# Attention and encoder in one kernel: a third exponential buffer, products with v in two halves, normalisation sums on GpSimd

## What is computed

```python
score = einsum('bhsd,bhtd->bhst', qh, kh) / sqrt(8)
attn = softmax(score, axis=-1)
a = einsum('bhst,bhtd->bhsd', attn, vh)      # then [b, 128, 512] reshaped to [b, 512, 128]
x = x + layernorm(a + XN)
```

## Time and profile before

| | us |
|---|---|
| median of three runs | 616.35 |
| the profiled execution | 617.56 |
| its span in the profile | 615.8 |
| TensorE matmul busy | 507.8 (82%) |
| VectorE busy | 525.9 (85%) |
| ScalarE busy | 395.2 (64%) |
| GpSimd busy | 194.5 (32%) |

### The profile page before, as it was taken

How to read it: one execution, slowest core, us unless ns; L and a number is a source line. 1 busy time by engine, 2 the same in 40 slices (tenths; PEclk the granted TensorE clock), 3 DMA queues, 4 the chain that set the end, 5 groups by cost and what they waited for, 6 DMA issues and landing times.

```text
span 615.8 us, 9778 instructions
## 1 busy us (share of the span) xinstructions
PE 507.8 (82%) x3468; PEld 196.9 (32%) x3475; DVE 525.9 (85%) x879; ACT 395.2 (64%) x773; POOL 194.5 (32%) x309
## 2 busy tenths in 40 slices
PE   1866999999999999999999998877578798888500
PEld 1634122222222222222222222256457665433200
DVE  5989799999999999999999994158988669899976
ACT  1753588989898889898888887534446321145252
POOL 7001021259321752045340338149366230000000
PEclk9999599999999999999999999999979799999965
DMA  8944010111220102211121200020000000001012
GB/s 215 304 142 141 17 40 25 36 30 36 70 71 24 41 22 75 56 46 30 33 58 49 60 19 7 6 81 2 2 2 1 1 1 1 1 0 35 2 34 68
DMA packets 31793, 28.94 MB, mean 47 GB/s; under 512 B 6256, under 2 KB 23800, under 8 KB 31744
## 3 DMA queue, kind: packets, MB, share of 16 engines
q1 hardware_dynamic: 29712, 27.33, 15.5%
q10 hardware_dynamic: 2032, 0.98, 0.6%
HBM read 19.23 MB, written 8.65 MB: 45 GB/s over the span
## 4 chain that ended last, share of the span: by engine, by line
PE 45%; DVE 30%; POOL 7%; ACT 6%; issue 4%; DMA 4%; SPq 2%; ACTq 1%; DVEq 0%
PE ps L1490 14%; PE ps L1485 11%; DVE row_max L1677 8%; PE ps L1458 5%; DVE space L925 4%; PE ps L584 2%; DVE space L861 2%; ACT attended L1619 2%; DMA w_in<-in_L_ffn_out_proj_w 1%; ACT space L1603 1%; PE ps L591 1%; DVE st L233 1%; DMA space<-max_turned 1%; ACT space L829 1%; POOL space L401 1%
## 5 line engine op out<-in xcount | busy, mean ns | idle before, releaser
L1677 DVE TENSOR_REDUCE row_max<-ps 128x2 f32<-128x1024 f32 x256 | 299.9, 1219 | 17.1 <-PE ps L1458 14.0
L1603 ACT ACTIVATE space<-ps 128x512 f32<-128x512 f32 x512 | 272.1, 604 | 49.3 <-PE ps L1485 48.8
L1485 PE MATMUL ps<-space 51*128 51x512 bf16 x512 | 158.5, 387 | 6.9 <-ACT space L1603 3.0
L1490 PE MATMUL ps<-space 128*32 128x512 f32 x1024 | 138.0, 611 | 2.9 <-ACT space L1603 0.7
L1458 PE MATMUL ps<-space 48*128 48x512 bf16 x512 | 125.5, 391 | 9.0 <-DVE row_max L1677 7.2
L1485 PEld LDWEIGHTS ps<-space 51*128 51x128 bf16 x512 | 40.8, 94 | 163.8 <-ACT space L1603 143.0
L1333 POOL CAST max_parts<-row_max 128x16 bf16<-128x16 f32 x32 | 6.4, 199 | 231.0 <-DVE row_max L1677 230.9
L584 PE MATMUL ps<-W,space 128*128 128x512 f32 x128 | 65.4, 592 | 0.4
L925 DVE TENSOR_REDUCE space<-ps 128x128 f32<-128x1024 f32 x32 | 38.7, 1220 | 9.7 <-PE ps L584 9.4
L447 POOL TENSOR_TENSOR space<-PC,same_row 128x512 f32<-128x512 f32 x32 | 33.0, 1063 | 35.7 <-DVE PC L875 27.6
L1458 PEld LDWEIGHTS ps<-space 48*128 48x128 bf16 x512 | 26.3, 94 | 49.1 <-DVE row_max L1677 41.0
(11 more groups left out here) (216 smaller groups left out, 624.7 us busy)
## 6 DMA issues: line engine op xcount, KB each, us to landing
space<-q_parts_dram SPq DMA_DIRECT2D x64, 48.0 KB
attended_dram<-attended SPq DMA_DIRECT2D x128, 18.0 KB
X<-in_L_attn_queries SPq DMA_DIRECT2D x8, 256.0 KB, 7.8
space<-in_L_ffn_w SPq DMA_DIRECT2D x2, 1024.0 KB, 6.5
space<-q_parts_dram SPq DMA_DIRECT2D x64, 32.0 KB
space<-attended_dram SPq DMA_DIRECT2D x16, 128.0 KB, 2.5
space<-inverses_dram SPq DMA_DIRECT2D x16, 128.0 KB
out<-space SPq DMA_DIRECT2D x4, 512.0 KB, 3.2
```

The source lines that it names most:

```text
L1485: pe.matmul(ps[:, col_bank(v), :], k_rows[rows_a, kappa // 4 % 2, tc * P:(tc + 1) * P], q_stack[rows_a, kappa % 4, b * S:(b + 1) * S], sta ...
L1490: mm = pe.matmul(ps[32 * m:32 * m + 32, PV, :], v_heads[:, tc, PAIR * (kappa // 4) + m % PAIR, :], probs[:, tc % 2, m, :], start=(tc == 0) ...
L1603: act.activation(probs[:, tc % 2, m, :], ps[:, col_bank(v), :], ACT.Exp, scale=1.0 / math.sqrt(DH)).then_inc(s_pr, 1)
L1677: dve.tensor_reduce(row_max[:, par].rearrange("p (a c) -> p a c", a=PAIR)[:, :, item], ring(n), AX.X, MAX).then_inc(s_free, 1)
```

## The change

`probs` becomes three buffers. TensorE's step moves column item 0 of the next block ahead of the first row products and pairs items 1 and 2; the products with v of a block are done one step later, in two halves of 256 columns (block 0 in one piece of 512), each behind a pair of row matmuls. ScalarE copies bank 7 of slot kappa - 1 after the second exponential of block 1 of slot kappa. Each piece of `first_group` comes one step earlier. SyncE does a slot's own loads first, then the denominators (c = 1), the attended values and the inverses' store (c = 2). For groups 0 and 1 GpSimd sums means and variances itself, by halving additions, in slots c = 5, 6, 8 and 9; group 2 keeps VectorE's bn_stats (at c = 5, and within `first_group_copies`).

```diff
-        probs = view(space4, 0, [2, QB, S])
+        probs = [view(space4, 0, [QB, S]), view(space4, QB * S, [QB, S]), view(space8, 0, [QB, S])]
...
+        def pool_add_up(pool, ch, src, scratch, total):
+            n = D // 2
+            ch.done(pool.tensor_tensor(scratch[:, :, 0:n], src[:, :, 0:n], src[:, :, n:2 * n], ADD))
+            ch.wait()
+            while n > 2:
+                n //= 2
+                ch.done(pool.tensor_tensor(scratch[:, :, 0:n], scratch[:, :, 0:n], scratch[:, :, n:2 * n], ADD))
+                ch.wait()
+            ch.done(pool.tensor_tensor(total.rearrange("p (b o) -> p b o", o=1), scratch[:, :, 0:1],
+                                       scratch[:, :, 1:2], ADD))
+            ch.wait()
+        def pool_centre(pool, ch, src, dst, scratch):
+            mean = smallp[:, 0, :]
+            pool_add_up(pool, ch, src, scratch, mean)
+            ch.done(pool.tensor_scalar(mean, mean, 1.0 / D, None, MUL))
+            ch.wait()
+            ch.done(pool.tensor_tensor(dst, src, over_f(mean), SUB))
+            ch.wait()
+            ch.done(pool.tensor_tensor(scratch, dst, dst, MUL))
+            ch.wait()
+        def pool_scale(pool, ch, dst, scratch):
+            var, inv = smallp[:, 2, :], smallp[:, 3, :]
+            pool_add_up(pool, ch, scratch, scratch, var)
+            ch.done(pool.tensor_scalar(var, var, 1.0 / D, EPS, MUL, ADD))
+            ch.wait()
+            ch.done(pool.tensor_tensor(inv, var, neg_half[:], ALU.pow))
+            ch.wait()
+            return pool.tensor_tensor(dst, dst, over_f(inv), MUL)
...
+        def pool_group(pool, ch, g, c):
+            scratch = XN[:, g]
+            if c == 4:
+                pool_divide(pool, ch, g)
+            if g < G - 2:
+                if c == 5:
+                    pool.wait_ge(s_r1, g + 1)
+                    pool_centre(pool, ch, A[:, g], A[:, g], scratch)
+                if c == 6:
+                    ch.done(pool_scale(pool, ch, A[:, g], scratch))
+                    ch.wait()
...
+            else:
+                if c == 6:
+                    pool.wait_ge(s_st, 1)
+                    ch.done(pool_norm(pool, ch, A[:, g], A[:, g]))
+                    ch.wait()
+                    pool_residual(pool, ch, g)
+                if c == 7:
+                    pool.wait_ge(s_st, 2)
+                    pool_norm(pool, ch, X[:, g], A[:, g]).then_inc(s_n2, 1)
+                    pool_out_bias(pool, g)
...
-            first_group(pe, 7)
...
+            def load_denominators(g):
 
                 for par in range(2):
                     sp.wait_ge(s_ast[par], 64 * 4 * (g + 1))
+                for h in range(NH // G):
+                    den = a_dram[:, g * (NH // G) + h:g * (NH // G) + h + 1, DH:DH + 1, :]
+                    sp.dma_start(den_sb[32 * h:32 * h + 32], den.rearrange("b h o (j f) -> (h o j) b f", f=D)).then_inc(s_dl, 16)
+            def load_attended(g):
...
+                if kappa + 1 < NQ:
+                    sp.wait_ge(s_pr, turn_item(kappa + 1) + 1)
+                    load_shift(kappa + 1)
                 if kappa:
                     sp.wait_ge(s_pve, kappa)
                     store_attended(kappa - 1)
 
-                if kappa + 1 < NQ:
-                    sp.wait_ge(s_pr, turn_item(kappa + 1) + 1)
-                    load_shift(kappa + 1)
             for kappa in range(NQ):
                 g, c = kappa // 8, kappa % 8
+                slot(kappa)
                 if c == 1 and g:
+                    load_denominators(g - 1)
+                if c == 2 and g:
                     load_attended(g - 1)
-                if c == 2 and g:
                     store_inverses(g - 1)
                 if c == 3 and g:
                     load_inverses(g - 1)
-                slot(kappa)
                 if 2 <= kappa < 2 + QB:
                     load_c(kappa - 2)
             sp.wait_ge(s_pve, NQ)
             store_attended(NQ - 1)
+            load_denominators(G - 1)
...
+                if g >= 2:
+                    pool_group(pool, ch, g - 2, c + 8)
                 if g:
-                    if c == 3:
-                        pool_divide(pool, ch, g - 1)
-                    if c == 5:
-                        pool_residual(pool, ch, g - 1)
-                    if c == 7:
-                        pool_input(pool, ch, g - 1)
+                    pool_group(pool, ch, g - 1, c)
...
-            def multiply_v(kappa, tc):
+            def multiply_v(n, half):
+                kappa, tc = n // TC, n % TC
+                if half == 0:
+                    if tc == 0 and kappa:
+                        pe.wait_ge(s_pve, kappa)
+                    pe.wait_ge(s_pr, column_item(kappa, tc, QB - 1) + 1)
+                if tc == 0 and half == 1:
+                    return
+                cols = slice(0, S) if tc == 0 else slice(half * S // 2, (half + 1) * S // 2)
                 for m in range(QB):
-                    mm = pe.matmul(ps[32 * m:32 * m + 32, PV, :], v_heads[:, tc, PAIR * (kappa // 4) + m % PAIR, :],
-                                   probs[:, tc % 2, m, :], start=(tc == 0), stop=(tc == TC - 1))
-                if tc == TC - 1:
+                    mm = pe.matmul(ps[32 * m:32 * m + 32, PV, cols], v_heads[:, tc, PAIR * (kappa // 4) + m % PAIR, :],
+                                   probs[n % 3][:, m, cols], start=(tc == 0), stop=(tc == TC - 1 and half == 1))
+                if tc == TC - 1 and half == 1:
                     mm.then_inc(s_pv, 1)
 
             pe.wait_ge(s_kl[0], 32)
 
             def step(kappa, tc):
 
-                piece = TC * (kappa - (NQ - 2)) + tc - 1
-                if piece >= 0:
-                    first_group(pe, piece)
-                n = 8 * (kappa + 2) + 2 * tc
+                n, row = TC * kappa + tc, 8 * (kappa + 2) + 2 * tc
                 ahead, following = kappa + 2 < NQ, kappa + 1 < NQ
                 score_columns(kappa, tc, 3)
                 if tc == 1 and following:
                     turn_max(kappa + 1)
+                score_columns(kappa, tc + 1, 0)
                 if ahead:
                     if tc == 0:
                         pe.wait_ge(s_ql[(kappa + 2) % 4], 96 * ((kappa + 2) // 4 + 1))
                         if (kappa + 2) % 4 == 0:
                             i = (kappa + 2) // 4
                             pe.wait_ge(s_kl[i % 2], 32 * (i // 2 + 1))
-                    score_rows(n, kappa + 2, 2 * tc)
-                score_columns(kappa, tc + 1, 0)
+                    score_rows(row, kappa + 2, 2 * tc)
+                    if n:
+                        multiply_v(n - 1, 0)
+                else:
+                    first_group(pe, TC * (kappa - (NQ - 2)) + tc)
                 score_columns(kappa, tc + 1, 1)
+                score_columns(kappa, tc + 1, 2)
                 if ahead:
-                    score_rows(n + 1, kappa + 2, 2 * tc + 1)
-                score_columns(kappa, tc + 1, 2)
-                if tc == 0 and kappa:
-                    pe.wait_ge(s_pve, kappa)
-                pe.wait_ge(s_pr, column_item(kappa, tc, QB - 1) + 1)
-                multiply_v(kappa, tc)
+                    score_rows(row + 1, kappa + 2, 2 * tc + 1)
+                else:
+                    multiply_v(n - 1, 0)
+                if n:
+                    multiply_v(n - 1, 1)
 
             for kappa in range(NQ):
                 for tc in range(TC):
                     step(kappa, tc)
+            for half in range(2):
+                multiply_v(TC * NQ - 1, half)
             back_end_pe(pe)
 
         @block.scalar
                 src = ps[0:PARTS * QB * TC, col_bank(v), 0:P // 2].bitcast(BF16)
                 act.copy(max_turned[:, kappa % 2, :], src).then_inc(s_pr, 1)
 
-            def exps(kappa, tc):
-                for m in range(QB):
+            def exps(kappa, tc, which=range(QB)):
+                for m in which:
                     v = column_item(kappa, tc, m)
                     act.wait_ge(s_sc, v + 1)
-                    act.activation(probs[:, tc % 2, m, :], ps[:, col_bank(v), :], ACT.Exp,
+                    act.activation(probs[(TC * kappa + tc) % 3][:, m, :], ps[:, col_bank(v), :], ACT.Exp,
                                    scale=1.0 / math.sqrt(DH)).then_inc(s_pr, 1)
 
-            copy_turned(0)
-            exps(0, 0)
-            for kappa in range(NQ):
-                for tc in range(1, TC):
-                    exps(kappa, tc)
-                    if tc == 1 and kappa + 1 < NQ:
-                        copy_turned(kappa + 1)
-                if kappa + 1 < NQ:
-                    exps(kappa + 1, 0)
+            def copy_attended(kappa):
                 act.wait_ge(s_pv, kappa + 1)
                 if kappa >= 2:
                     act.wait_ge(s_ast[kappa % 2], 64 * (kappa // 2))
                 act.copy(attended[:, kappa % 2, :], ps[:, PV, :]).then_inc(s_pve, 1)
+            copy_turned(0)
+            for kappa in range(NQ):
```

(65 more changed lines are left out.)

## The result

The changed kernel takes 628.52 us in the median of four runs (625.19 to 630.14), the kernel before 616.57 (616.21 to 618.8): ratio 1.0163, 95% interval 1.0132 to 1.0195. Timed again in three rounds on another occasion it is 629.84 against 617.59, ratio 1.0185 (1.0128 to 1.0243). The sign was forecast, the size was not: +12 us against +4.6, and the time lies outside the stated range of 603 to 627 us.

A forecast was written before the change was run, and what follows sets the result against it. The order of work, not an engine's busy time, was taken as the bound; slots +10.4, start -1.2, last two slots -5.2 and encoder +0.6 gave +4.6 us, so 621.0 us, range 603 to 627.

The forecast's parts named there:

- The slot: Attention slots: each takes 10.48 us, 0.54 above 9.94; over 29 slots this adds 10.4 us against 293.5.
- both places: Two stretches of each slot: the copy's chain before block 2's column item 0, 2.37 us; block 0's whole product with v, 2.61.
- The price of a half: TensorE's product with v in a half of 256 columns: 0.57 us, each half paying entry and exit anew.
- the five ordinary segments: The rest of a slot outside its two lossy stretches, from row products to row products: 1.10 us each, 5.50 together.
- rival B: VectorE bounds the slot: without the copy's loss 9.70 us and 598.4 in all, without both losses 9.13 and 582; chance 0.13.
- The 5.3 us of the crowded slots is counted as gone: Slots where the group before is finished: their extra 5.3 us over 29 times 9.94 disappears entirely.
- Start, -1.2: Slot 0 starts without a product with v, so it ends 1.2 us earlier; bounds 0 and -3.
- Last two slots, -5.2: From column item 3 of slot 30 to the encoder's first product: 23.1 us instead of 28.3.
- Encoder, +0.6: After the encoder's first product the denominators reach VectorE 7.5 us later instead of 6.9; bounds 0 and 2.
- Rival A: Halves of the product with v cost 0.50 us, without a drain: slot 10.09, time 609.7 us; chance 0.16.
- C: GpSimd's centring or scaling takes 2 us over the free 9.4, making eight slots late: 626 us; chance 0.08.
- D: The change of order does nothing by itself, losses and gains at the slots' ends being equal: 616 us; chance 0.07.

The follow-up runs named there:

- the later copy: The changed kernel with ScalarE's copy of bank 7 moved one exponential later, behind exponential 2 of block 1: 608.75 us, ratio 0.985 to the kernel before.
- the part for TensorE and ScalarE alone: The changed kernel's TensorE and ScalarE orders and three buffers, with GpSimd, SyncE and VectorE working for finished groups as in the kernel before: 633.7 us, ratio 1.0264.

## Why the prediction was right or wrong

By its own steps, against the first profile after, whose span is 11.0 us longer where the sum had 4.6:

- *The slot.* Right in its mechanism and nearly in its size. The chain shows both places, with 2.38 and 2.61 us for 2.37 and 2.61; the later copy removes 0.79 us at the first (0.78 was the difference worked out), and moving both gives 9.44. The wait of VectorE of 1.02 us once a slot is there. The price of a half, 0.57, is as taken. The Trainium skill, page TensorEngine Tiling (Array Packing), section Key Properties, states that changing the tiling mode drains TensorE. The trace agrees in that each half pays for the change of shape anew, 0.31 us from the row matmul to its first round and 0.33 from its second round to the column item. The slot is 0.09 longer than 10.48, or 0.63 above 9.94 where 0.54 was forecast. The 0.09 lies in the five ordinary segments, of which the sum had 1.10 each: four take 1.11 and one 1.15 from row products to row products. In the longer one C0 of the next slot, which also waits for the DMA of the maxima, starts 0.05 after its pair. Times 29 the 0.09 is 2.6 us. The 9.13 that rival B gives for a slot without both losses, by VectorE, was not reached: with both gone TensorE's own work takes 9.44.
- *"The 5.3 us of the crowded slots is counted as gone."* This failed by 1.4 us: VectorE's inversion exceeds the room and costs 0.46 in three slots. The sums on GpSimd were sized well: a centring 8.2 us for 8.1, a scaling 7.9 for 7.4, both hidden, and no split late in the changed kernel.
- *Start, -1.2.* Not seen: slot 1 starts at 79.6 in both first profiles. The granted clock ahead of it was nearly the same in these two (0.69 and 0.66), which speaks against a gain of 1.2. But the start varies by more than that from run to run (78.3 to 82.5 over all eleven profiles, experiments included), so the term isn't settled.
- *Last two slots, -5.2.* It was -4.0: 24.3 us from C3 of slot 30 to the encoder for 23.1. Steps of 2.70 (2.68 taken) are right, but three things were missed. The first piece waits 1.29 us for the last reduction, where 0.7 was taken, because VectorE does group 2's statistics in slot 29, a stall that I had called room: with the part for TensorE and ScalarE alone, where they stand in slots 28 and 30, this wait is 0.52 us. One step of slot 31 takes 3.08, since C2 waits there for an exponential behind the copy, and the copy's chain in slot 30 costs 0.2 more than taken.
- *Encoder, +0.6.* 215.1 us from its first product to the end, before 214.4: +0.7. But the second profiles of the two kernels have 214.6 and 212.8, so it lies within the variation.

So 2.6 + 1.4 + 1.2 + 1.2 us were missing. The steps that failed are the size of the slot (10.57 for 10.48, the largest share because it counts 29 times), the crowded slots' 5.3 us counted as gone (1.4 stay), the start's -1.2 (nothing seen), and the last two slots (24.3 for 23.1, over half of it the last reduction's wait). All err in one direction, and a forecast of +4.6, the difference of +10.4 and -5.8, more than doubles by them. The loop of the slot, on which the sign depends, held. Rival A (no drain) fell by the halves' 0.57, B by the copy's chain, C by the hidden sums, D by the slot of 10.57.

## What to carry to other kernels

When an engine works by a written order, follow each wait to what stands ahead of its releaser on the other engine: a copy put one exponential too early cost about 21 us here (629.84 against 608.75, or 1.0185 and 0.985 of the kernel before). Then moving the product with v while the copy still stood ahead of an exponential gained nothing in a slot; moving both gained 0.34 us. And each shorter slot bares work that the longer one had covered (here GpSimd's copies and VectorE's inversion). A forecast that is the difference of a loss and a gain deserves a range from the errors of both.

## What the runs showed of the hardware

A change between products in row groups and products of all rows in column groups costs TensorE about 0.10 us going in (0.31 us from the second of a pair of row matmuls to a product with v, where a pair otherwise takes 0.22) and 0.11 coming out (0.33 behind a round of 256 columns, which takes 0.22; 0.55 behind one of 512, which takes 0.43), for 256 columns as for 512. VectorE starts reductions of 1024 elements 1.13 us apart while each is shown as 1.22 long. And over the 14 us at the start of the attention the granted clock of one and the same kernel was 0.66 in one run and 0.50 in another (the changed kernel), 0.69 and 0.81 (the kernel before); slot 0 was about 2 us longer at the lower value of each pair.
